# First layer and attention block of a transformer kernel joined into one program section

## The reference

```python
# first layer: 16 heads of 16 features over time 512, x (256, 512) per batch
attn = softmax(where(kv_mask, (q * scale) @ k, -inf))
mean = attn @ v ; std = sqrt(relu(attn @ (v * v) - mean * mean))
xn   = masked_instance_norm(x, mask)
x    = (xn * std + mean) * mask
# block: 16 heads of 32 features, 256 rows of 512
x = x + attention(layernorm(x) @ w_qkv + b_qkv, ltor_mask) @ w_ao + b_ao
x = x + attention(layernorm(x) @ w_q, encoder_states @ w_kv, cross_mask) @ w_co + b_co
x = x + gelu(layernorm(x) @ w1 + b1) @ w2 + b2
```

## Time and profile before

| | |
|---|---|
| median of 3 runs | 1916.93 us (1914.57 to 1919.9) |
| profiled execution | 1918.11 us |
| its span | 1916.3 us |
| TensorE busy | 1756.7 us (92%) |
| VectorE busy | 1346.0 us (70%) |
| ScalarE busy | 1065.7 us (56%) |
| GpSimd busy | 347.4 us (18%) |
| mean granted clock | 0.962 |

### The profile page before, as it was taken

How to read it: one execution, slowest core, us unless ns; L and a number is a source line. 1 busy time by engine, 2 the same in 40 slices (tenths; PEclk the granted TensorE clock), 3 DMA queues, 4 the chain that set the end, 5 groups by cost and what they waited for, 6 DMA issues and landing times. The chain is left out here.

```text
span 1916.3 us, 33999 instructions
## 1 busy us (share of the span) xinstructions
PE 1756.7 (92%) x12216; PEld 1178.8 (62%) x12216; DVE 1346.0 (70%) x2802; ACT 1065.7 (56%) x2399; POOL 347.4 (18%) x397
## 2 busy tenths in 40 slices
PE   5999999999999982789999989999999789999998
PEld 2333333333333320578888877788888579999998
DVE  4678788887878751589999888989999753233332
ACT  1555665666566561477777877777777561111111
POOL 0001111211111122222332222222223040000000
PEclk9899999999999985899999989999999889999999
DMA  4001011110100001322333243333333150000000
GB/s 153 25 21 47 16 46 27 36 48 15 46 15 25 23 18 44 105 67 67 73 82 80 67 128 99 91 83 89 84 84 90 34 175 12 11 11 11 11 11 23
DMA packets 74102, 105.01 MB, mean 55 GB/s; under 512 B 21344, under 2 KB 36192, under 8 KB 73440
## 3 DMA queue, kind: packets, MB, share of 16 engines
q1 hardware_dynamic: 63456, 82.08, 15.5%
q0 software_dynamic: 8192, 16.79, 3.7%
q10 hardware_dynamic: 2304, 4.20, 0.8%
HBM read 39.55 MB, written 4.72 MB: 23 GB/s over the span
## 5 line engine op out<-in xcount | busy, mean ns | idle before, releaser
L416 DVE TENSOR_REDUCE nmax<-ps 128x2 f32<-128x1024 f32 x256 | 311.2, 1220 | 136.1 <-PE ps L314 135.2
L548 ACT ACTIVATE prob<-ps 128x1024 f32<-128x1024 f32 x256 | 261.9, 1023 | 223.7 <-PE ps L326 223.4
L1183 ACT ACTIVATE at_prob<-at_t,at_nmax 128x256 f32<-128x256 f32 x512 | 256.3, 505 | 102.1 <-DVE at_nmax L1008 95.9
L341 PE MATMUL ps<-prob,v 128*64 128x512 f32 x1024 | 285.8, 638 | 0.0
L1008 DVE CUSTOM_DVE_ANT_0 at_t<-at_t,at_off 128x256 f32<-128x256 f32 x512 | 238.2, 502 | 8.8
L314 PE MATMUL ps<-k,q 32*128 32x512 f32 x1024 | 194.7, 459 | 17.9 <-DVE k L404 7.9
L314 PEld LDWEIGHTS ps<-k,q 32*128 32x128 f32 x1024 | 84.4, 190 | 191.6 <-issue 108.9
L1483 ACT ACTIVATE mlp_h<-ps,b 128x256 f32<-128x256 f32 x128 | 53.7, 472 | 266.6 <-PE ps L1418 266.5
L1003 DVE SCALAR_TENSOR_TENSOR at_t<-ps,at_mask 128x512 f32<-128x512 f32 x256 | 175.0, 684 | 19.3 <-PE ps L851 18.7
L1522 DVE CAST mlp_h_hi<-mlp_h 128x512 fp32r<-128x512 f32 x64 | 30.5, 476 | 218.4 <-ACT mlp_h L1483 218.3
L1321 POOL TENSOR_TENSOR at_low<-at_low,at_high 128x512 fp32r<-128x512 f32 x64 | 82.6, 1291 | 500.6 <-DVE at_high L1031 500.6
(11 more groups left out here) (165 smaller groups left out, 4032.6 us busy)
## 6 DMA issues: line engine op xcount, KB each, us to landing
at_k_stack<-at_high SPq DMA_DIRECT2D x256, 64.0 KB, 2.5
at_q_stack<-at_high SPq DMA_DIRECT2D x128, 64.0 KB, 2.7
at_q_stack<-at_high POOLq DMA_DIRECT2D x128, 64.0 KB, 2.4
at_q_stack<-at_low SPq DMA_DIRECT2D x128, 64.0 KB, 2.1
at_k_stack<-at_low POOLq DMA_DIRECT2D x128, 64.0 KB, 2.4
mlp_w_in<-in_w SPq DMA_DIRECT2D x32, 256.0 KB, 3.0
c_in<-in_ctx SPq DMA_DIRECT2D x8, 512.0 KB, 4.3
X<-in_x SPq DMA_DIRECT2D x8, 512.0 KB, 5.0
```

The lines of the kernel that those rows point to most:

```text
L341: mm = eng.matmul(ps[2 * QD * k:2 * QD * (k + 1), VB, :], v[:, c, HG * G + 2 * p + k, :], prob[:, M % PROBS, k, :], start=(c == 0), stop=( ...
L416: eng.tensor_reduce(nmax[:, n % 2, j, 2 * p:2 * p + 2], ps[:, at:at + 2, :], AX, ALU.max, negate=True).then_inc(s_max, 1)
L548: eng.activation(prob[:, M % PROBS, :, :], ps[:, ST:ST + 2, :], ACT.Exp).then_inc(s_exp, 1)
L1183: ins = eng.activation(prob[:, m % 2, i, :], t[:, p, i, :], ACT.Exp, scale=-1.0, bias=nmax[:, m % 4, i:i + 1], accum_out=z[:, T % 2, j, 2 ...
```

## The change

The two sections become one: `layer0` and `attention` return, for each engine, functions that write its instructions, and a single `nc.Block()` calls them: the first layer, with a function `lead` of the block called in every step, then `runs`, with a function `late` of the first layer called in each step of a run. With step = 8 (w - 32) + s:

- TensorE issues the two turn_x in steps -4 and -2, and q0, k0, v0, v1, q1 as halves in steps 0, 1, 3 to 10. ScalarE takes x in steps -3 and -1. These items now use bank 7, the first layer's item bank.
- SP issues the stacks of q0 and k0 at w = 33, after a wait for the last turned scores; q1's after shares_in of batch 7 and ahead of its shares_out; k1's and wo_raw after it.
- Batch 6 is finished from the end of the layer to step 6 of run 0; batch 7 from step 1 of run 0 to step 15, with finish_x on GpSimd in its list for run 1.
- ScalarE waits at the weight pieces of wo (now steps 13 to 15 of run 0) for all finishing of the first layer.
- Roots for the first layer norm are computed for batches 0 to 4 in the first layer and for 5 to 7 in run 3.
- The cross attention's rows of b_row, its first mask and context are loaded ahead of run 2's stacks, after a wait for the maxima of runs 0 and 1.
- Tiles are placed in another order in SBUF, some shared by both parts, and `gate` waits guard their reuse.

```diff
+        g["gates"] = {
+            "loads": [(s_big, 6 * DMA)],
+            "turn before last": [(s_free, number[("turn", GROUPS - 2)] + 1)],
+            "last turn": [(s_free, number[("turn", GROUPS - 1)] + 1)],
+            "maxima": [(s_max, 8 * GROUPS)],
+            "turned scores": [(s_st, 8 * GROUPS)],
+            "values out": [(s_vout, 2 * GROUPS)],
+            "regroups": [(s_re[k], regrouped(2 * GROUPS - 1, k)) for k in range(OUTS)],
+            "finished": [(s_fin, FINISH * NB)],
+        }
...
+        normal_x(LAST - 1)
+
+        def late(run, m):
+
+            if (run, m) == (0, 1):
+                shares(LAST)
+            if run == 0 and m in (4, 6):
+                last_mask(LAST - 1, m // 2 - 2)
+            if (run, m) == (0, 8):
+                positive_variance(LAST)
+            if (run, m) == (0, 10):
+                normal_x(LAST)
+            if run == 0 and m in (14, 15):
+                last_mask(LAST, m - 14)
...
+        roots(LAST - 1)
+
+        def late(run, m):
+
+            if (run, m) == (0, 6):
+                mean_squared(LAST)
+            if (run, m) == (0, 9):
+                roots(LAST)
...
+        def late(run, k):
+
+            if (run, k) == (0, 1):
+                finish_x(LAST - 1, 0)
+                finish_x(LAST - 1, 1)
+            if (run, k) == (0, 3):
+                finish_shares(LAST, 0)
+                finish_shares(LAST, 1)
+                finish_variance(LAST)
+            if (run, k) == (1, 1):
+                finish_x(LAST, 0)
+                finish_x(LAST, 1)
...
-    SC, PT, OB, IB, TB = 0, 2, 4, 6, 7
+    SC, PT, OB, IB, TB = 0, 2, 4, 7, 6
...
+    LOT = 5
+    LOTS = {1: (LOT - 2, 0, LOT, NB), 2: (NB - 2, 1, 0, NB - 2), 3: (NB + 1, 1, NB - 2, NB)}
...
-             7: ((2, 0), (2, 1)), 8: ((2, 2),), 9: ((2, 3),), 10: ((3, 0),), 11: ((3, 1),), 12: ((3, 2),), 13: ((3, 3),)}
+             7: ((2, 0), (2, 1)), 8: ((2, 2),), 9: ((2, 3),), 13: ((3, 0),), 14: ((3, 1),), 15: ((3, 2), (3, 3))}
...
+        def lead(w, after):
+
+            if (w, after) == (G0 + 1, False):
+                gate(eng, "turned scores")
+                stack(eng, 0, "q", 0, (0, 1))
+                stack(eng, 0, "k", 0, (0, 1))
+            if (w, after) == (G0 + 2, False):
+                stack(eng, 0, "q", 1, (0, 1))
+
+        def runs():
+
+            stack(eng, 0, "k", 1, (0, 1))
+            eng.dma_start(wo_raw[:], d["wo_self"]).then_inc(s_wo, DMA)
+            for run in range(1, RUNS):
+                if run == 2:
+                    gate(eng, "finished")
+                    eng.wait_ge(s_max, 2 * STEPS)
+                    eng.dma_start(b_cross[:], d["b_row"][:, 2:4, :]).then_inc(s_rows, DMA)
+                    load_mask(0)
+                    load_context(0)
...
+        def lead(w, s, after):
+
+            step = 8 * (w - G0) + s
+            if not after:
+                if step == 2:
+                    taken(eng, "q", 0, 0)
+                return
+            if step in (-4, -2):
+                turn_x(0, (step + 4) // 2)
+            if step == 0:
+                gate(eng, "loads")
+            if step == 3:
+                gate(eng, "last turn")
+            ahead = {0: 0, 1: 1, 3: 2, 4: 3, 5: 4, 6: 5, 7: 6, 8: 7, 9: 8, 10: 9}
+            if step in ahead:
+                item(*AHEAD[ahead[step] // 2], 0, (ahead[step] % 2,))
+
+        def runs():
+
+            gate(eng, "maxima")
...
+            if step == -34:
+                variances(0, 0, 0, LOT)
+            if step == -17:
+                reciprocals(0, 0, 0, LOT)
+            if step == -6:
                 layer_norm(0)
+            if step == 2:
                 high_parts(0, "q", 0)
+            if step == 3:
+                gate(eng, "loads")
                 mask_off(0)
+            if step == 5:
+                high_parts(0, "k", 0)
+            if step in (6, 8):
+                values(0, (step - 6) // 2)
...
+            if step == -29:
+                roots(0, 0, 0, LOT)
+            if step == -3:
+                gate(eng, "loads")
+            if step in (-3, -1):
+                take_x(0, (step + 3) // 2)
+            if step == 1:
                 take("q", 0, 0)
+            if step == 4:
                 take("k", 0, 0)
...
                     if c == 0 and layer == 0 and role == 3:
                         eng.wait_ge(s_wo, DMA)
+                gate(eng, "finished")
```

More of the change, by code:

```diff
@@ new lines, in gpsimd, with runs @@
+    def gpsimd(eng):
+        def runs(late):
+            for run in range(RUNS):
+                for n in range(2):
+                    for k in range(2):
+                        if run:
+                            eng.wait_ge(s_score, STEPS * (run - 1) + 8 * n + 8)
+                        eng.wait_ge(s_hi, 4 * run + 2 * n + k + 1)
+                        eng.tensor_tensor(low[:, k, :, :], low[:, k, :, :].bitcast(F32), high[:, k, :, :].bitcast(F32),
+                                          ALU.subtract).then_inc(s_lo, 1)
+                        if (run, n, k) == (0, 0, 0):
+                            gate(eng, "turned scores")
+                        stack(eng, run, "qk"[k], n, (2,))
+                        late(run, 2 * n + k)
+        return runs
@@ L1598, in build, with _ @@
             keep(attentions, "w_lo", [P, DC, 3 * D], F32R)
[L1599 to L1604 removed]
+            keep(attentions, "b_self", [P, 2, D])
+            keep(attentions, "mask_self", [P, SB, S])
+            keep(attentions, "z0", [P, NH * D // P])
+            keep(attentions, "x_mean", [P, NB, SB])
+            keep(attentions, "x_var", [P, NB, SB])
+            keep(attentions, "six", [P, 6])
+            keep(attentions, "two", [P, 2])
+            first, then = layer0(nc, d, g), attention(nc, d, g)
+            with nc.Block() as block:
+                @block.sync
+                def _(eng):
+                    lead, runs = then["sync"](eng)
+                    first["sync"](eng, lead)
+                    runs()
+                @block.tensor
+                def _(eng):
+                    lead, runs = then["tensor"](eng)
+                    first["tensor"](eng, lead)
+                    runs()
+                @block.vector
+                def _(eng):
+                    lead, runs = then["vector"](eng)
+                    late = first["vector"](eng, lead)
+                    runs(late)
+                @block.scalar
+                def _(eng):
+                    lead, runs = then["scalar"](eng)
+                    late = first["scalar"](eng, lead)
+                    runs(late)
+                @block.gpsimd
+                def _(eng):
+                    late = first["gpsimd"](eng)
+                    then["gpsimd"](eng)(late)
         mlp(nc, d, g)
```

1754 lines of the change are left out of this document (870 added, 884 removed).

## The result

The changed kernel takes 1910.11 us (median of 20 runs, 1903.11 to 1917.83), the kernel before 1919.89 in as many runs (1914.57 to 1926.95). The ratio is 0.995, with a 95% interval of 0.9936 to 0.9964: faster by some 10 us, just past the 0.3% that a measurement of this kernel can tell. The forecast was 1909, that is 8 us under the 1916.93 that the first three runs of the kernel before had given. The profiled execution has a span of 1908.9 us, against 1916.3.

What follows compares the result with a forecast made beforehand. TensorE bounds run 1, several engines run 0, and dependency chains the 35.4 us gap between layer and block. Terms -41.3 - 1 + 2 + 13 + 17 + 2 = -8.3 us give 1909, own range 1902 to 1916.

Steps and rivals of the forecast that it cites:

- Ahead of step 0: First layer's end: added turns and takes of x and a layer norm cost +3 us (0 to 5).
- Interleaved steps: Layer's last steps with half projections, ten at 3.57 us on TensorE: step 11 starts 38.2 us after step 0.
- The rival in which the clock falls in there: Interleaved steps: four at half clock add 14 us, giving 1923; chance 0.08.
- First scores: Block's start: scores come 50.6 us after step 0 instead of 94.9, TensorE idle some 9 us while SP issues stacks.
- Runs 0 and 1: Block's first two runs: work moved in for batches 6 and 7 costs net +13 us (7 to 20).
- -1 for q's second half: Block's start: q's second half no longer lies between the first scores and the third, gaining another 1 us.
- The wait ahead of run 2: Before scores(2, 0): stack DMAs queue behind SP's wait for maxima; TensorE idles 13 to 14.5 us, 17 with clock.
- cheap wait: Rival: the 17 us ahead of run 2 fall away, giving 1892; chance 0.18.
- Run 3: Roots of batches 5 to 7 with two table loads lengthen this run by +2 us (1.5 to 3).
- The wait for "finished": Rival at step 13 of run 0: ScalarE's wait is the barrier again, 1915; about 3 us margin counted; chance 0.10.
- One mark: Sign for runs 0 and 1: together about 111 us instead of 97.6; prediction wrong if over 120.
- the second rival: Run 0 stretched by GpSimd passes holding VectorE: 1924; decided from some 125 us between maxima; chance 0.14.

Runs made afterwards that it cites:

- e9_kept_busy: Changed kernel with three loads behind run 2's stacks, batch 6 finished in the layer's last steps, nine unused matmuls in the idle before first scores: 1892.57 us, ratio 0.9859.
- e1_loads_after: Changed kernel with SP's wait for the maxima of runs 0 and 1 and its three loads moved behind run 2's stacks: 1891.45 us, ratio 0.9868.
- e5_k_stack_on_scalar: Changed kernel with the 8 DMAs of k's first stack issued by ScalarE beside SP's 8 for q: 1910.36 us, ratio 0.9969.
- e8_short_and_early: Changed kernel with loads behind run 2's stacks, batch 6 finished early, batch 7's GpSimd passes on 16 of 512 columns, its roots as copies: 1884.54 us, ratio 0.9834.
- run 4: Not a follow-up experiment: a stretch of the block within each kernel, after run 3; runs are numbered from 0 and cut at their first maxima.
- e6_early_and_split: Changed kernel with loads behind run 2's stacks, batch 6 finished in the layer's last steps, k's first stack issued by ScalarE: 1890.01 us, ratio 0.9853.

## Why the prediction was right, step by step

The median is 1910.11 where 1909 was forecast, and the terms are mostly those of the sum. They are taken from the two first profiles. The forecast was -8 us against a median of three runs that the later 20 put 3 us higher; against those the change measured -9.8.

- **Ahead of step 0**: from the turn item of group 30 to step 0 the kernel before took 10.2 us and the changed one 11.6, so +1.4 for a forecast of +3.
- **Interleaved steps**: 38.4 us to step 11 for 38.2, at a clock of 1.00. The rival in which the clock falls in there did not come.
- **First scores**: 51.05 us after step 0 for 50.6, with 9.72 us idle for "some 9", ended by the k stack's DMA as named. From step 0 to the first scores 43.9 us are gained (94.9 - 51.05), less 1.4: 42.5, where the sum had 41.3.
- **Runs 0 and 1** without the idle time: 64.1 + 60.6 - 12.9 = 111.8 us against 54.8 + 42.2 = 97.0, so +14.8. The sum had +13 for moved work, +2 for the clock and -1 for q's second half, together +14. The 7.5 us of locked VectorE were 7.7, and taking the passes away made run 0 shorter by 4.5 to 5.6 us. The split among the terms is less sure than their sum: the +2 for the clock after the gap is about 1.5 or less by e9_kept_busy, and of ScalarE's 5 us, taken at some 3, the two table loads make up 2.6 and cost 0.1 to 1.3 in run 0 and nothing over runs 0 and 1. The -1 for q's second half was not tried. k's second stack, 4 us later, cost nothing: TensorE has no idle time ahead of it in run 0 of the changed kernel.
- **The wait ahead of run 2**: 12.9 us of idle time, where 13 to 14.5 were forecast. From the end of the maxima (861.7) to scores (2, 0) it was 13.4 us, for 13.1 to 13.5 in the sum, but TensorE had work for half a us of it. With run 2's +2.2 that makes 15.1 by the profile, and 18.5 by the medians of e1_loads_after; 17 was written. The rival "cheap wait" was wrong: TensorE ran out of work 0.5 us after those maxima ended.
- **Run 3**: 46.4 us for a forecast of 45, so +3.6 where +2 was written. I carried the +2.6 of run 6 over at a discount. It was the term most wrong in proportion. It was 44.8 in e5_k_stack_on_scalar and e8_short_and_early, as in run 6; why it varies is open.
- **Runs 0 to 3 together**: 216.1 - 182.6 = +33.5 us, for the sum's 13 + 2 - 1 + 17 + 2 = 33.
- **The wait for "finished"** at step 13 is no barrier. GpSimd's last pass ends at 808.1, and ScalarE's first piece of wo stands at 813.42: 5 us of margin, where 3 were counted.

Two things stood in no term, and nearly cancelled in the profiled pair: the first layer was 7.4 us longer up to the turn item of group 30, and everything from run 4 on 6 us shorter. Both are of the size of the scatter between profiles: the turn item lies between 675.6 and 687.7, and the time from run 4's first maxima to the end between 939.4 and 949.5 us (941.7 in the changed kernel's first profile, 947.6 before). That the span of one profile agrees with the sum is therefore partly luck; that the 20-run medians differ by 9.8 us is not.

**One mark was wrong as written.** "Runs 0 and 1 together about 111 us instead of 97.6, wrong if over 120" speaks of the distance between first maxima. But the idle time ahead of scores (2, 0) lies inside that distance, since run 2's first maxima come after it. It measured 124.7, which is past the mark, with 111.8 of it without the idle time. The sum was right and the mark contradicted it. The same slip sits in the point of decision of the second rival (125 us): the forecast itself, with its wait ahead of run 2, would have reached it. Without the idle time the runs took 111.8, some 13 us under 97.6 + 27.

## What to carry to other kernels

When a barrier is replaced by gates, look for each new wait at what is queued behind it on the same issuer: here three loads not needed for six runs had been put ahead of 16 stack DMAs, and behind a wait that ends when they are due, which gave back 14 to 18.5 of the 42 us won. Moving them behind those DMAs, and finishing the last but one batch in the steps where VectorE is idle, gives 1886.66 us, 1.6% under the kernel before; the first of the two alone gave 1.3%. Work on GpSimd that lay under an idle stretch comes into VectorE's way once the stretch gets shorter, so a saving ahead of it is first to be checked against what the stretch covered.

## What the runs showed of the hardware that was not expected

- The first layer up to the turn item of group 30, the same work for TensorE in all kernels, ended anywhere between 675.6 and 687.7 us in the profiles of this study, and at 680.4 and 687.7 in two executions of one kernel. In the changed kernel's first profile the delay came in steps of 1.5 to 3.4 us at single groups. What starts them was not tried.
- The granted clock behind the first 5 us of run 0 was 0.76 to 0.86 whether TensorE had stood still for 9.8 us ahead of the run or worked at a clock of 1.00; TensorE was busy for 6.4 to 6.6 of the first 10 of these us. In run 1 of e1_loads_after it was 1.00 with 6.78 of 10 us busy.
- A VectorE operation with a single SBUF input of 128x2 took 1.27 us for 0.17 beside a GpSimd pass of 2.85 us.
- Two queues issue DMAs side by side, but each slower than alone: 8 DMAs took 6.07 us on ScalarE's queue and 5.8 on SP's, where SP alone needed 5.03 to 5.14 for 8. In e6_early_and_split it was 6.38 and 5.84.
